# Decoder layer with a two-of-eight expert stage: reads of the first gathers' columns, the order of the last W2 loads, one expert's subtraction on GpSimd, and reads of tile numbers, moved

## The chip, the cores and the metric

The kernel runs on one core of one Trainium2 chip. The metric is the time on the device in microseconds (us). The engines are named as in the profile: PE (TensorE), PEld (its weight loads), DVE (VectorE), ACT (ScalarE), POOL (GpSimd) and SP (SyncE). SP issues most of the DMAs; POOL issues the gathers and scatters.

## The reference, cut to what matters

Eight batches of 256 rows of 256 numbers pass through three residual stages. The third one is the subject here.

```python
x = x + rbf_attention(layernorm(x))                 # self-attention, exp(-distance^2), softmax over it
x = x + cross_attention(ctx, ctx, layernorm(x))     # 16 heads, mask
xs = layernorm(x).reshape(-1, 256)                  # 2048 tokens
weights, sel = top_k(xs @ Wg, 2)                    # 2 of 8 experts for each token
weights = softmax(weights)
h = relu(einsum('td,edf->etf', xs, W1) + b1)        # W1: 8 x 256 x 1024
out_e = einsum('etf,efd->etd', h, W2) + b2          # W2: 8 x 1024 x 256
x = x + sum_k weights[k] * out_e[sel[k]]
```

## The kernel before

The program has an attention part and an expert part, and each engine's program is written out in the order in which it runs. The first part (`attention`) is called for steps -1 to 9. Each step works on several of the eight batches at different stages: scores of one batch, exponentials of the one before it, and so on. Steps 8 and 9 (`choosing` and `placing` in the code) have no new batch, and beside the last attention work they sort the tokens of the first five batches (10 groups of 128) into tiles of 128 rows for one expert each.

This sorting runs on DVE as a chain. `routing_table(core, eng, 0, c)` for c = 0 to 3 builds comparison matrices (L1800 to L1810, `local_hot`, `row_hot`, `local_vals`, `tile_vals`), nearly all of them from two inputs in SBUF. After each, PE multiplies them (`table_product`, L1561). The four PE products stand at fixed places between the attention's own products, and PE does nothing behind one of them until it has run. After the fourth, `routing_index` (L1823 to L1854) turns the sum into the rows to be gathered and raises the event `idx`.

The expert part (`experts`) has 39 tiles. Step n works on tile n-1 (the gathered rows are transposed, `ex_rows_t`, L2022), tile n-2 (times W1, `ex_hidden`, L2058 on PE; relu and rounding on ACT, L2068 and L2075; the rest after rounding, `hid_lo`, on DVE, L2078) and tile n-3 (times W2, `ex_out`, L2099). POOL gathers the rows of tiles 0 to 3 ahead (`ex_gather`, a copy L1993 and an indirect DMA L1996) and adds the results to the output one tile after another (`ex_scatter`, L2011). Step 0 to 17 are written out, then follows a loop. The second part of the tokens (the last three batches) is sorted in steps 3 to 11, beside the first tiles. `prefix_product` (L1551) in step 4 is the first PE instruction of it, and needs the choice of experts of the last batch, made on DVE (`st_router`, `st_best`, `routing_choice`; the last result is `both`, L1612).

A product with W2 takes W2 in two parts, the rounded number (`hi`) and what is left over (`lo`). Each expert's W2 (1 MB) is loaded by SP (`load_expert`, L490, in the order 0, 1, 2, 3, 7, 4, 5, 6, each one waiting for the load two before it), copied rounded by ACT (L1508) and subtracted by DVE (L1513) over 2048 numbers in each partition. The subtraction of expert 0 is done by POOL instead, in eight pieces of 256 (L1497), two in each of four attention steps. `ex_out` of tiles 0 to 2 waits for as many finished experts as the table `tile_splits` says, and tile 3 waits for all eight.

Which expert a tile has, which column of the table it uses and how many splits it needs is read from SBUF into a register (`value_load`, shown as TENSOR_LOAD in the lists below). An engine's following instructions wait in its program until the number is there. The reads stand right ahead of the instruction that uses the number.

## Time and profile before

| | |
|---|---|
| median of 3 runs | 641.94 us (641.94, 637.71, 984.14) |
| the profiled execution, its time | 641.79 us |
| its span, first to last instruction | 640.1 us |
| mean granted TensorE clock | 0.976 |
| PE busy | 583.3 us (91%) |
| DVE, ACT, POOL busy | 369.1, 333.6, 220.6 us |
| chain that ended last | PE 47%, DMA 31%, DVE 8%, issue 5% |

The attention part ends at about 354 us of the span, and the expert part fills the rest. "Granted clock" is the share of the full PE clock (1.00 is 2.4 GHz, 0.50 is 1.2 GHz). In the rows of a timeline the first number is the start of an instruction or a group in us from the span's start, the second its length in us; in brackets stands how long the engine was idle ahead of it and what ended that.

### The profile page before, as it was taken

What the parts mean: (1) busy time and instruction counts of PE and PEld (TensorE: products, weight loads), DVE (VectorE), ACT (ScalarE), POOL (GpSimd) and SP (SyncE); (2) the same over time, 40 slices, a digit from 0 to 9 for tenths busy, and PEclk for the clock granted to TensorE, in tenths of its full rate; (3) what the DMA queues carried; (4) which work ended last, traced back from release to release, by engine and by line L of the source; (5) the groups of instructions that cost most, each with busy time, mean ns of one, the idle gap of its engine ahead of it and who ended that gap; (6) DMA issues with size and microseconds to landing.
All of it is one profiled execution on the core that took longest, in us unless ns stands there. A gap on an engine that the chain in (4) does not pass through costs nothing.

```text
span 640.1 us, 15134 instructions
## 1 busy us (share of the span) xinstructions
PE 583.3 (91%) x4812; PEld 537.3 (84%) x4852; DVE 369.1 (58%) x920; ACT 333.6 (52%) x787; POOL 220.6 (34%) x283
## 2 busy tenths in 40 slices
PE   4666899999999999998968799999999999999991
PEld 3565888889798888977756799999999999999991
DVE  3636867778676767757868777565233332323331
ACT  4432364655547456453455664555656556565550
POOL 8322212212213121111002616443454655545532
PEclk9979999999999999999969899999999999999996
DMA  7383909063370907346157955666667676766732
GB/s 222 101 95 89 116 3 107 13 80 72 42 110 1 148 4 87 66 52 100 44 183 270 335 169 167 167 176 221 179 197 215 176 225 174 217 190 192 217 86 25
DMA packets 55430, 85.34 MB, mean 133 GB/s; under 512 B 6416, under 2 KB 44144, under 8 KB 55376
## 3 DMA queue, kind: packets, MB, share of 16 engines
q1 hardware_dynamic: 46368, 73.59, 48.3%
q0 software_dynamic: 7616, 10.26, 8.6%
q10 hardware_dynamic: 1392, 0.79, 0.4%
q8 instruction: 32, 0.52, 0.3%
q14 instruction: 22, 0.18, 0.1%
HBM read 62.44 MB, written 9.31 MB: 112 GB/s over the span
## 4 chain that ended last, share of the span: by engine, by line
PE 47%; DMA 31%; DVE 8%; issue 5%; ACT 2%; POOL 2%; POOLq 2%; SPq 1%; DVEq 0%; ACTq 0%
DMA out<-y,scatter_now 26%; PE bank L998 14%; PE bank L2058 5%; PE bank L1310 4%; PE bank L1253 4%; PE bank L1339 4%; PE bank L2099 4%; PE bank L1307 3%; PE bank L1250 3%; DMA q_stack<-cq_lo 2%; PE bank L964 2%; DMA exp_ring<-L_attn_Wo 1%; DMA experts_w<-L_ffn_W 1%; SPq L1081 1%; DMA slots_in<-xn_rows,gather_now 1%
## 5 line engine op out<-in xcount | busy, mean ns | idle before, releaser
L2058 PE MATMUL bank<-slots_t,w_now 128*128 128x128 f32 x1248 | 147.3, 277 | 0.0
L2058 PEld LDWEIGHTS bank<-slots_t,w_now 128*128 128x128 f32 x1248 | 144.0, 194 | 0.0
L2068 ACT ACTIVATE hid<-bank,b_tile 128x128 f32<-128x128 f32 x312 | 88.9, 368 | 55.1 <-PE bank L2058 55.1
L2011 POOL DMA_INDIRECT out<-y,scatter_now x39 | 63.7, 1633 | 119.4 <-DMA out<-y,scatter_now 77.5
L2078 DVE TENSOR_TENSOR hid_lo<-hid,hid_hi 128x1024 fp32r<-128x1024 f32 x39 | 47.8, 1226 | 97.1 <-ACT hid_hi L2075 97.1
L2099 PE MATMUL bank<-experts_w,hid_hi 128*128 x624 | 83.5, 285 | 2.5 <-ACT hid_hi L2075 1.5
L1261 DVE TENSOR_REDUCE row_max<-bank 128x2 f32<-128x512 f32 x128 | 81.0, 681 | 7.2 <-PE bank L1253 6.4
L1322 ACT ACTIVATE exp_ring<-bank 128x512 f32<-128x512 f32 x128 | 67.7, 605 | 26.3 <-PE bank L1310 26.3
L2099 PEld LDWEIGHTS bank<-experts_w,hid_hi 128*128 128x128 f32 x624 | 76.5, 188 | 2.8 <-issue 2.7
L1253 PE MATMUL bank<-k_stack,q_stack 96*128 96x256 f32 x256 | 67.3, 377 | 2.2 <-DMA q_stack<-cq_lo 2.2
L1310 PE MATMUL bank<-q_stack,k_stack 98*128 98x256 f32 x256 | 67.0, 382 | 0.0
L1310 PEld LDWEIGHTS bank<-q_stack,k_stack 98*128 98x128 f32 x256 | 51.3, 200 | 3.5
L1253 PEld LDWEIGHTS bank<-k_stack,q_stack 96*128 96x128 f32 x256 | 50.2, 196 | 3.5
L897 POOL TENSOR_SCALAR rstd<-moments 128x2 f32<-128x2 f32 x24 | 7.8, 326 | 128.7 <-DVE moments L894 128.7
L2075 ACT ACTIVATE hid_hi<-hid 128x512 fp32r<-128x512 f32 x78 | 49.3, 633 | 4.7
L1996 POOL DMA_INDIRECT slots_in<-xn_rows,gather_now x39 | 41.0, 1052 | 25.8 <-POOL gather_now L1993 15.4
L1993 POOL COPY gather_now<-gather_idx 128x1 uint32 x39 | 41.6, 1067 | 10.7 <-DVE jump L1854 10.7
L1307 PE MATMUL bank<-mask_k,ident_bf 128*128 128x512 bf16 x112 | 44.5, 398 | 0.0
L2099 PE MATMUL bank<-experts_w,hid_lo 128*128 x312 | 43.1, 280 | 0.0
L2028 ACT ACTIVATE slots_t<-bank 128x256 f32<-128x256 f32 x39 | 15.0, 384 | 53.5 <-PE bank L2022 53.5
L1250 PE MATMUL bank<-mask_q,ident_bf 128*128 128x512 bf16 x105 | 40.9, 390 | 0.1
L2099 PEld LDWEIGHTS bank<-experts_w,hid_lo 128*128 128x128 f32 x312 | 39.5, 188 | 0.0
(276 smaller groups left out, 1023.0 us busy)
## 6 DMA issues: line engine op xcount, KB each, us to landing
w_now<-L_ffn_W SPq DMA_DIRECT2D x39, 1024.0 KB
experts_w<-L_ffn_W SPq DMA_DIRECT2D x8, 1024.0 KB, 7.6
k_stack<-ck_hi SPq DMA_DIRECT2D x32, 128.0 KB, 4.6
q_stack<-cq_hi SPq DMA_DIRECT2D x32, 128.0 KB, 6.8
ctx_in<-ctx SPq DMA_DIRECT2D x8, 256.0 KB, 7.7
k_stack<-ck_lo SPq DMA_DIRECT2D x16, 128.0 KB, 4.8
q_stack<-cq_lo SPq DMA_DIRECT2D x16, 128.0 KB, 7.6
out<-x SPq DMA_DIRECT2D x7, 256.0 KB, 7.5
```

The costliest lines, as they stand in the source:

```text
L998: mm = eng.matmul(out, a, b, start=start and i == 0, stop=stop and i == len(terms) - 1, skip_group_check=skip)
L1250: eng.matmul(ps[:, :], core.ident_bf[:, :], core.mask_q[:, :, :], start=True, stop=False, skip_group_check=True)
L1253: mm = eng.matmul(ps[:, qt * S:(qt + 1) * S], q_stack[0:QROWS, c, i, qt * P:(qt + 1) * P], k_stack[0:QROWS, i, :], start=False, stop=True, ...
L1261: core.e["maxed"].at(eng.tensor_reduce(core.row_max[:, :, h], ps[:, :].rearrange("p (t k) -> p t k", t=KT), AX.X, ALU.max))
L1307: eng.matmul(ps[:, :], core.ident_bf[:, :], core.mask_k[:, :, :], start=True, stop=False, skip_group_check=True)
L1310: mm = eng.matmul(ps[:, kt * S:(kt + 1) * S], core.k_stack[b.p][0:rows, i, kt * P:(kt + 1) * P], core.q_stack[b.p][0:rows, c, i, :], start ...
L1322: core.e["exp"].at(eng.activation(core.exp_ring[:, n % 8, :, :], ps[:, :], ACT.Exp, scale=HD ** -0.5))
L2011: core.rows_out.at(eng.indirect_dma_start(core.out_rows, bass.IndirectOffsetOnAxis(ap=core.scatter_now[b.p][:, :], axis=0), core.y[b.p][:, ...
L2058: mm = eng.matmul(banks[half][:, f * P:(f + 1) * P], core.w1_now[b.p][:, c, start:start + P], core.slots_t[b.p][:, c, :], start=c == 0, st ...
L2068: act = eng.activation(core.hid[:, g, :], banks[half][:, f * P:(f + 1) * P], ACT.Relu, bias=core.b1_tile[b.p][:, g:g + 1])
L2075: core.m["hid_hi"].at(eng.activation(core.hid_hi[b.p][:, part, :], core.hid[:, part, :], ACT.Copy))
L2099: mm = eng.matmul(ps[:, 0:D], left[b.p][:, f, :], core.experts_w[:, bass.ds(x * PLACE + (part * FT * D + f * D), D)], start=term == 0 and ...
```

## The change

Four things are moved; none changes what is computed, and the count of heavy instructions is the same except that one subtraction of 2048 becomes eight of 256.

- POOL reads the columns of the first four gathers after the event `order` (raised in step 8) rather than one by one behind `idx`.
- SP loads W2 of expert 7 ahead of W1 of tile 1. The loads of W2 of experts 4, 5 and 6 wait until the gathers of tiles 0 and 1 have landed.
- W2 of expert 1 is subtracted on POOL in eight pieces in attention step 9, no longer on DVE behind `routing_index`. ACT's and DVE's work on W2 of expert 4 moves from step 2 and the head of step 3 to a place behind `ex_hidden` of tile 1, right ahead of that of expert 5.
- PE reads the tile's numbers for `ex_out` at the head of a step from 3 on (not in the loop).

```diff
--- before.py
+++ after.py
@@ -787,7 +787,10 @@
     exps(2, 2, 3, 4)
     at(0, st_rbf_out)
     if name == "gpsimd" and 3 <= it.v < 7:
-        split_first(core, eng, 2 * (it.v - 3))
+        split_piece(core, eng, 0, 2 * (it.v - 3))
+    elif name == "gpsimd" and placing:
+        for piece in range(PIECES):
+            split_piece(core, eng, 1, piece)
     exps(2, 5, 6)
     if choosing and name == "tensor":
         prefix_product(core, eng, 0)
@@ -825,7 +828,6 @@
         routing_table(core, eng, 0, 2)
         routing_table(core, eng, 0, 3)
         routing_index(core, eng, 0)
-        split_expert(core, name, eng, 1)
     scores(1, 4, 5)
     at(0, st_project, "cq")
     at(-1, st_transpose, "xnT")
@@ -857,7 +859,7 @@
         elif placing:
             split_expert(core, name, eng, 3)
     elif name == "gpsimd" and 3 <= it.v < 7:
-        split_first(core, eng, 2 * (it.v - 3) + 1)
+        split_piece(core, eng, 0, 2 * (it.v - 3) + 1)
     scores(0, 0, 1, 2)
     at(3, st_best)
     if choosing and name == "vector":
@@ -1461,11 +1463,13 @@
     e.wait_ge(core.r["order"], 1)
     e.wait_ge(core.E["residual_early"], 16 * EARLY_BATCHES)
     ex_load(core, "sync", e, Step(0, 0))
+    core.e["t_tile"].wait(e, LAST_BATCH)
+    load_expert(core, e, 7)
     e.wait_ge(core.r["table"], 4)
     ex_load(core, "sync", e, Step(0, 1))
-    core.e["t_tile"].wait(e, LAST_BATCH)
-    load_expert(core, e, 7)
     core.e["p_hT"].wait(e, LAST_BATCH)
+    for b in range(2):
+        core.rows_in.wait(e, Step(0, b))
     for x in (4, 5, 6):
         load_expert(core, e, x)
 
@@ -1489,11 +1493,11 @@
     return core.experts_w[:, start:start + FT * D]
 
 
-def split_first(core, eng, piece):
+def split_piece(core, eng, x, piece):
 
     width = FT * D // PIECES
-    hi, lo = (expert_part(core, 0, part)[:, piece * width:(piece + 1) * width] for part in range(2))
-    eng.wait_ge(core.w2["hi"], 1)
+    hi, lo = (expert_part(core, x, part)[:, piece * width:(piece + 1) * width] for part in range(2))
+    eng.wait_ge(core.w2["hi"], x + 1)
     rest = eng.tensor_tensor(lo, lo.bitcast(F32), hi.bitcast(F32), ALU.subtract)
     if piece == PIECES - 1:
         rest.then_inc(core.w2["lo"], 1)
@@ -1508,8 +1512,8 @@
         eng.activation(hi, lo.bitcast(F32), ACT.Copy).then_inc(core.w2["hi"], 1)
     elif name == "vector":
         eng.wait_ge(core.w2["hi"], n + 1)
-        if n == 1:
-            eng.wait_ge(core.w2["lo"], 1)
+        if n == 2:
+            eng.wait_ge(core.w2["lo"], 2)
         eng.tensor_tensor(lo, lo.bitcast(F32), hi.bitcast(F32), ALU.subtract).then_inc(core.w2["lo"], 1)
 
 
@@ -1871,9 +1875,11 @@
             at(0, ex_load)
     elif name == "gpsimd":
         if n == 0:
-            eng.wait_ge(core.r["idx"], 1)
+            eng.wait_ge(core.r["order"], 1)
+            core.columns = [column_of(core, eng, Step(b // 2, b % 2)) for b in range(4)]
             for b in (3, 4):
                 core.xn_stored.wait(eng, Step(b // 2, b % 2))
+            eng.wait_ge(core.r["idx"], 1)
         if n == FIRST:
             eng.wait_ge(core.r["idx"], 2)
             for b in (6, 7):
@@ -1891,6 +1897,10 @@
     elif name == "tensor":
         if n == 1:
             st_output(core, name, eng, LAST_BATCH, it)
+        if n is not None and n >= 3 and it.back(3).inside(MAX_TILES):
+            expert_of(core, eng, it.back(3))
+            if n < 6:
+                core.splits = splits_of(core, eng, it.back(3))
         at(1, ex_rows_t)
         at(2, ex_hidden)
         if n == 2:
@@ -1911,9 +1921,8 @@
         elif n == 4:
             split_expert(core, name, eng, 6)
         at(2, ex_hidden)
-        if n == 2:
+        if n == 3:
             split_expert(core, name, eng, 4)
-        elif n == 3:
             split_expert(core, name, eng, 5)
         if n == 2:
             store_residual(core, eng, LAST_BATCH)
@@ -1931,10 +1940,9 @@
             split_expert(core, name, eng, 3)
             st_normalise(core, name, eng, LAST_BATCH, it, 2)
             split_expert(core, name, eng, 7)
-        elif n == 3:
-            split_expert(core, name, eng, 4)
         at(2, ex_hidden)
         if n == 3:
+            split_expert(core, name, eng, 4)
             split_expert(core, name, eng, 5)
             st_router(core, name, eng, LAST_BATCH, it)
             st_best(core, name, eng, LAST_BATCH, it)
@@ -1968,6 +1976,10 @@
     return x
 
 
+def splits_of(core, eng, b):
+    return eng.value_load(core.tile_splits[0:1, bass.ds(b.v, 1)], min_val=1, max_val=NE)
+
+
 def tile_number(core, eng, b):
     return eng.value_load(core.tile_expert[0:1, bass.ds(b.v, 1)], min_val=0, max_val=NE - 1)
 
@@ -1989,7 +2001,7 @@
     rows, now = gather_buffers(core, b)
     before = b.back(4 if isinstance(b.v, int) and b.v < 6 else 2)
     core.rows_in.wait(eng, before, apart=core.apart)
-    g, col = column_of(core, eng, b)
+    g, col = core.columns[b.v] if isinstance(b.v, int) and b.v < 4 else column_of(core, eng, b)
     core.m["gnow"].at(eng.tensor_copy(now[:, :], core.gather_idx[g][:, bass.ds(col, 1)]))
     core.m["gnow"].wait(eng, b, apart=core.apart)
     core.m["xT"].wait(eng, before, apart=core.apart)
@@ -2084,8 +2096,7 @@
     if name == "tensor":
         x = expert_of(core, eng, b)
         if isinstance(b.v, int) and b.v < 3:
-            splits = eng.value_load(core.tile_splits[0:1, bass.ds(b.v, 1)], min_val=1, max_val=NE)
-            eng.wait_ge(core.w2["lo"], splits)
+            eng.wait_ge(core.w2["lo"], core.splits)
         elif isinstance(b.v, int) and b.v == 3:
             eng.wait_ge(core.w2["lo"], NE)
         core.m["hid_hi"].wait(eng, b)
```

The lists that follow show each engine's program by position, with the events that an instruction waits for. Line numbers of the changed kernel are 2 to 12 higher than those of the kernel before, and L2xxx, L1501 and L1517 there are the same code as L1497 and L1513 here.

POOL's program at the end of attention step 9, before. `rstd` is the last layernorm work of the attention steps (batch 6), `tile_col` the table of columns, `gather_now` and `slots_in` are the gather's index and its rows; the second to fourth gather repeat the last five rows.

```order
L897 TENSOR_SCALAR rstd<-moments 128x2 [waits e_ln2_stats]
L899 TENSOR_TENSOR rstd<-rstd,minus_half 128x2 [waits e_ln2_eps]
L1978 TENSOR_LOAD tile_col [waits xn_stored0,xn_stored1,r_idx]
L1978 ISA x2
L1993 ISA
L1993 COPY gather_now_154<-gather_idx_204 128x1
L1996 DMA slots_in_148<-xn_rows,gather_now_154 128x256 [waits m_gnow]
```

The same place in the changed kernel.

```order
L899 TENSOR_SCALAR rstd<-moments 128x2 [waits e_ln2_stats]
L901 TENSOR_TENSOR rstd<-rstd,minus_half 128x2 [waits e_ln2_eps]
L1501 TENSOR_TENSOR experts_w<-experts_w 128x256 [waits w2_hi] x8
L1990 TENSOR_LOAD tile_col [waits r_order]
L1990 ISA x2
...
L1990 TENSOR_LOAD tile_col
L1990 ISA x2
L2005 ISA [waits r_idx,xn_stored0,xn_stored1]
L2005 COPY gather_now_154<-gather_idx_204 128x1
L2008 DMA slots_in_148<-xn_rows,gather_now_154 128x256 [waits m_gnow]
```

Eight pieces of the subtraction now stand between the layernorm work and the gathers, four reads of `tile_col` (two of them shown) behind them, and `idx` is waited for only ahead of the copy.

DVE's program in expert steps 2 and 3, before, without the reads of tile numbers. The `experts_w` rows are, from the top, the subtractions of experts 4 and 5; `hid_lo_214` and `hid_lo_215` belong to tiles 0 and 1; `logits`, `top_54` and `idx_55` to the choice of the last batch.

```order
L2078 TENSOR_TENSOR hid_lo_214<-hid,hid_hi_134 128x1024 [waits m_hid_hi]
...
L2044 COPY b_tile_152<-b_cols 128x8
L1513 TENSOR_TENSOR experts_w<-experts_w 128x2048 [waits w2_hi]
L2078 TENSOR_TENSOR hid_lo_215<-hid,hid_hi_135 128x1024 [waits m_hid_hi]
L1513 TENSOR_TENSOR experts_w<-experts_w 128x2048 [waits w2_hi]
L1436 COPY logits<-bank 128x16 [waits e_p_gate]
L1592 MAX top_54<-logits 128x8 [waits e_gate]
L1592 MAX top_54<-logits 128x8
L1595 MAX_INDEX idx_55<-top_54,logits 128x8 [waits e_best] x2
```

And in the changed kernel.

```order
L2090 TENSOR_TENSOR hid_lo_214<-hid,hid_hi_134 128x1024 [waits m_hid_hi]
...
L2056 COPY b_tile_152<-b_cols 128x8
L2090 TENSOR_TENSOR hid_lo_215<-hid,hid_hi_135 128x1024 [waits m_hid_hi]
L1517 TENSOR_TENSOR experts_w<-experts_w 128x2048 [waits w2_hi] x2
L1438 COPY logits<-bank 128x16 [waits e_p_gate]
L1596 MAX top_54<-logits 128x8 [waits e_gate]
L1596 MAX top_54<-logits 128x8
L1599 MAX_INDEX idx_55<-top_54,logits 128x8 [waits e_best] x2
```

The subtraction of expert 4 has gone from ahead of tile 1's `hid_lo` to behind it, so that both stand between it and the last batch's choice. On ACT the rounding of expert 4 moves in the same way, from behind tile 0's `hid_hi` to behind tile 1's.

PE's program from the end of step 2 to the first `ex_out`, before. L1416 is the transposing of the last batch's `xn_ffn` for the router, L1431 the router, the `ident,slots_in` rows transpose tile 2, `slots_t_151,w_now` is tile 1 times W1.

```order
L1416 MATMUL bank<-ident,xn_ffn 128x128 [waits e_ln2,e_hT_lo]
...
L2022 MATMUL bank<-ident,slots_in_142 128x128 [waits m_slots_t,rows_in2]
L2022 MATMUL bank<-ident,slots_in_142 128x128
L2058 MATMUL bank<-slots_t_151,w_now_213 128x128 [waits m_slots_t,w1_in1]
L2058 MATMUL bank<-slots_t_151,w_now_213 128x128 x15
L1431 MATMUL bank<-gate_w,xf_t 128x8 [waits e_xfT]
...
L1972 TENSOR_LOAD tile_expert
L1972 ISA x2
L2087 TENSOR_LOAD tile_splits
L2087 ISA x2
L2099 ISA [waits m_hid_hi,w2_lo]
```

And in the changed kernel.

```order
L1418 MATMUL bank<-ident,xn_ffn 128x128 [waits e_ln2,e_hT_lo]
...
L1984 TENSOR_LOAD tile_expert
L1984 ISA x2
L1980 TENSOR_LOAD tile_splits
L1980 ISA x2
L2034 MATMUL bank<-ident,slots_in_142 128x128 [waits m_slots_t,rows_in2]
L2034 MATMUL bank<-ident,slots_in_142 128x128
L2070 MATMUL bank<-slots_t_151,w_now_213 128x128 [waits m_slots_t,w1_in1]
L2070 MATMUL bank<-slots_t_151,w_now_213 128x128 x15
L1433 MATMUL bank<-gate_w,xf_t 128x8 [waits e_xfT]
...
L2110 ISA [waits m_hid_hi,w2_lo]
```

The two reads have moved from between the router and tile 0's product with W2 to ahead of tile 2's transposes. The steps behind it are changed in the same way.

## Rows read from the trace of the kernel before

**Rows 1.** Busy time by stretch: us, PE, PEld, DVE, ACT, POOL, PEclk, DMA share, GB/s

```profile
320.00:330.00 10.00, 4.24 (x26) 3.93 (x26) 5.02 (x26) 4.56 (x4) 0.00 (x0) 0.65 0.54 176
330.00:340.00 10.00, 10.00 (x73) 7.90 (x76) 9.83 (x31) 5.98 (x12) 1.60 (x2) 0.84 0.81 246
500.00:620.00 120.00, 120.00 (x1053) 120.00 (x1052) 39.77 (x73) 69.34 (x199) 62.13 (x70) 1.00 0.68 192
```

**Rows 2.** Timeline in the loop: PE, the W1 products of two tiles that follow each other

```profile
505.18 3.74 PE L2058 MATMUL bank<-slots_t,w_now 128*128 128x128 f32 x32
...
511.80 3.74 PE L2058 MATMUL bank<-slots_t,w_now 128*128 128x128 f32 x32
```

**Rows 3.** Timeline, DVE, the last three routing tables of step 9 and what follows

```profile
335.76 1.55 DVE L1810 TENSOR_TENSOR tile_vals<-onehot,local_vals 128x400 fp32r<-128x400 f32 x3
337.22 0.73 DVE L917 TENSOR_SCALAR xn_ffn<-x,moments,rstd 128x256 f32<-128x256 f32 x2
...
342.12 1.55 DVE L1810 TENSOR_TENSOR tile_vals<-onehot,local_vals 128x400 fp32r<-128x400 f32 x3
...
345.82 0.17 DVE L1854 COPY jump<-taken 128x8 f32<-128x8 f32 x1
345.90 2.29 DVE L1513 TENSOR_TENSOR experts_w<-experts_w 128x2048 fp32r<-128x2048 f32 x1
```

**Rows 4.** Timeline, PE, the third and fourth table product

```profile
341.20 0.72 PE L1561 MATMUL bank<-tile_vals,row_hot 128*128 128x240 f32 x5
...
343.73 0.82 PE L1561 MATMUL bank<-tile_vals,row_hot 128*128 128x240 f32 x5 [0.38 <-DVE tile_vals L1810]
```

**Rows 5.** Line L1497 (POOL's pieces of expert 0), and POOL's last attention instruction

```profile
L1497 POOL TENSOR_TENSOR experts_w<-experts_w x8: 716/726/741, 125.9 to 256.8; 128x256 fp32r<-128x256 f32 x8
...
335.53 0.78 POOL L899 TENSOR_TENSOR rstd<-rstd,minus_half 128x2 f32<-128x2 f32 x1
```

**Rows 6.** Timeline, places where POOL and DVE both read SBUF with two inputs

```profile
25.86 1.27 POOL L925 TENSOR_TENSOR x<-x,bias_attn_bo 128x512 f32<-128x512 f32 x1 [5.66 <-DVE bias_attn_bo L688]
26.22 1.45 DVE L628 TENSOR_TENSOR xattnWvl<-exp_ring,xattnWvh 128x512 fp32r<-128x512 f32 x1
...
27.60 0.68 DVE L628 TENSOR_TENSOR xattnWol<-exp_ring,xattnWoh 128x512 fp32r<-128x512 f32 x1
...
347.00 1.24 POOL L1993 COPY gather_now<-gather_idx 128x1 uint32 x1 [10.70 <-DVE jump L1854]
```

**Rows 7.** Timeline, PE: one product at the low clock, the last attention product, tiles 0 and 1

```profile
329.21 0.63 PE L998 MATMUL bank<-xattnWoh,tr_hi 128*128 128x256 f32 x2
...
352.99 0.40 PE L998 MATMUL bank<-xattnWoh,tr_lo 128*128 128x256 f32 x2
...
354.11 0.44 PE L2022 MATMUL bank<-ident,slots_in 128*128 128x128 f32 x2 [0.71 <-DMA slots_in<-xn_rows,gather_now]
...
356.02 0.44 PE L2022 MATMUL bank<-ident,slots_in 128*128 128x128 f32 x2 [1.48 <-DMA slots_in<-xn_rows,gather_now]
```

**Rows 8.** Chain that ended last, in order of time: tile 1's gather

```profile
350.14 5.84 DMA slots_in<-xn_rows,gather_now
```

**Rows 9.** Timeline of all engines, from the last batch's layernorm to tile 1's W2 product

```profile
359.05 0.73 DVE L917 TENSOR_SCALAR xn_ffn<-x,moments,rstd 128x256 f32<-128x256 f32 x2 [0.94 <-POOL rstd L899]
...
368.45 2.26 PE L2099 MATMUL bank<-experts_w,hid_hi 128*128 x16 [1.55 <-ACT hid_hi L2075]
...
368.82 0.63 ACT L2075 ACTIVATE hid_hi<-hid 128x512 fp32r<-128x512 f32 x1
369.36 1.90 ACT L1508 ACTIVATE experts_w<-experts_w 128x2048 fp32r<-128x2048 f32 x1
...
374.97 0.21 DVE L1612 TENSOR_TENSOR both<-onehot 128x48 f32<-128x48 f32 x1
...
376.86 2.46 PE L2099 MATMUL bank<-experts_w,hid_hi 128*128 x16 [0.92 <-issue]
```

**Rows 10.** DMA issues of 356 to 360 us: the last W2 load, KB, us to landing

```profile
experts_w<-L_ffn_W SPq DMA_DIRECT2D x1, 1024.0 KB, 6.4
```

## The prediction

> **What bounds the kernel now.** I read the busy time by stretch first, to see which engine is full where. From 500 to 620 us PE is busy throughout at a granted clock of 1.00 [rows 1], and two W1 products of tiles that follow each other start 6.62 us apart [rows 2]: in the expert part PE sets the pace, and a us that the first tiles start earlier or later is a us at the end. In the 20 us from 320 PE is neither full nor at its full clock (4.24 of 10 us busy, clock 0.65, then 0.84) [rows 1]. So I read the timelines of all engines from there to about 380 us, where everything that the change touches stands.
>
> Three waits of PE are what the change is about. (a) Tile 0's and tile 1's transposes wait 0.71 and 1.48 us for gathered rows [rows 7]; tile 1's gather takes 5.84 us to land [rows 8]. (b) Tile 0's product with W2 starts 1.55 us after PE's last work, where two numbers are read; for tile 1 the gap is 0.92 us [rows 9]. (c) Ahead of both, PE's third and fourth table product depend on DVE: the fourth starts at 343.73, 0.38 us late, right behind DVE's last `tile_vals`, which end at 343.67 [rows 3, 4].
>
> **Reading the columns ahead.** DVE raises `idx` at 345.99, POOL's first copy starts at 347.00 and ends at 348.24 [rows 3, 6]. The read costs about 1.0 us there. The copy itself, of one number in each partition, takes 1.24 us because DVE's subtraction of expert 1 runs from 345.90 to 348.19 [rows 3]: POOL is let through when that ends. With both gone a copy would end near 346.3, and the gathers start up to 1.9 us earlier. What this can give is bounded by wait (a): 0.71 + 1.48 = 2.2 us on PE.
>
> **W2 loads behind the gathers.** They leave the gathers more of the DMA engines. The last W2 load takes 6.4 us to land [rows 10]. Loads 4 and 5 would start when tile 1's rows are in, at the latest at 356.0 in before's time [rows 8], and 6 when 4 is in, so all have landed by about 356.0 + 2 x 6.4 = 368.8. ACT needs 4 only after tile 1's `hid_hi`, which ends at 369.45 now [rows 9]. I cost this at nothing; if the loads took twice as long, ACT's splits would be up to 5 us late.
>
> **The eight pieces on POOL.** This is the term that decides. They stand behind `rstd`, which ends at 336.31 [rows 5], and take 0.726 us each [rows 5], 5.8 us together. POOL is idle then, so by busy time they are free. But DVE has no gap between 335.76 and 343.67 [rows 3], and nearly all of it is comparisons and products with two inputs in SBUF. What happens when both engines do that is seen at 26.22: a DVE subtraction that takes 0.68 us when it is alone takes 1.45 us, while POOL's L925 runs until 27.13 [rows 6]. DVE lost 0.77 us of the 0.91 us that POOL still had. Eight pieces taken in turn with DVE's instructions then cost DVE 0.726 - 0.14 = 0.59 us each, 4.7 us; taken one behind the other 5.8 us. I take 5.3. PE waits for these very tables, and its other work cannot pass a table product, so PE's fourth table product, `idx` and all behind them are 5.3 us later.
>
> One row speaks against it: POOL's `rstd` power (335.53 to 336.31, two SBUF inputs of two numbers) runs beside three `tile_vals` from 335.76, which take their usual 1.55 us [rows 3, 5]. It reads only two numbers, and a piece reads 256, as L925 reads 512; I side with L925.
>
> The Trainium skill (SBUF — State Buffer, "Who interferes with whom") says that a DVE instruction with two SBUF inputs and a GpSimd instruction that reads SBUF exclude each other for the whole instruction, whichever starts first. The row at 26.22 agrees and the row at 335.53 does not. By this rule alone the term would be the full eight pieces, 5.8 us, and by the row at 335.53 alone nothing.
>
> **The clock.** In the 20 us in which PE first idled the granted clock was 0.65 and 0.84 [rows 1]; the same pair of products takes 0.63 us at the low level (1.2 GHz) and 0.40 at 2.4 GHz [rows 7]. PE's third table product can now start 5.3 us later than 341.20 [rows 4], an idle stretch like that one. Between the fourth table product and the last attention product, 343.73 to 353.39 [rows 4, 7], PE has some 6 us of work on the path, with waits for ACT and DVE between. At the low clock throughout it grows by up to 4.9 us (0.8 of it); if the clock stays high, nothing. I take 1.7, about a third of the work at the low level.
>
> **DVE without expert 1's subtraction.** It ended at 348.19 [rows 3], 0.15 us ahead of which `r_heads` could have run: -0.15 us.
>
> **From the last attention product to tile 1's W2 product** (353.39 to 376.86 [rows 7, 9]). With the rows there in time, tile 0's W1 product starts 1.7 us earlier: transposes, ACT's copy and transposes take 1.2 us, where it is 2.9 us now. But what PE does next, transposing the last batch's `xn_ffn`, waits for DVE, which ends that at 359.78 [rows 9], and no part of the change moves this. Behind it stand now the two reads, 1.5 us by the gap in (b), so that tile 2's transposes and tile 1's W1 product start 0 to 0.5 us earlier than now. Gain (a) ends there. ACT finishes tile 1's `hid_hi` 1.7 to 2.1 us earlier than 369.45 [rows 9], since expert 4 is not ahead of it. Then come ACT's roundings of 4 and 5 (1.90 us each [rows 9]), and DVE's subtractions (2.29 us each [rows 3]) with the choice of the last batch behind both. In sum: 367.3 to 367.8, two roundings later 371.1 to 371.6; DVE's first subtraction ends at 371.5 to 372.0, the second at 373.8 to 374.3, `both` 1.6 us later at 375.4 to 375.9, against 375.18 now. PE's prefix product waits for it, takes 0.76, and tile 1's product with W2 follows without the gap, at 376.2 to 376.7, against 376.86. So gains (a) and (b), 2.2 + 1.55 + 0.92 = 4.7 us as they stand in the rows, shrink to about 0.4 us: what is late next is DVE with expert 4 and 5 ahead of the choice.
>
> **Reads further on.** From tile 2 on the gaps are not there, since PE has products queued; they cost nothing before and nothing after. The loop is not touched.
>
> **Sum.** 5.3 + 1.7 - 0.15 - 0.4 = +6.45 us. The profiled execution's 641.79 (span 640.1) is 0.15 below the median, so the median should be 641.94 + 6.45 = 648.4 us. With the low ends, 4.7 + 0 - 0.15 - 0.65, it is 645.8, with the high ends, 5.8 + 4.9 - 0.15 - 0.2, 652.3.
>
> **Rivals.**
> 1. DVE is not held up: both read side by side as at 335.53, or DVE always goes first and POOL's pieces fill its gaps. Side by side: -0.15 - 0.4 gives 641.4 us. DVE first: the pieces start at 343.7, end near 349.6, and tile 1's gather lands about 1.5 us later than 355.98, of which the wait for `xn_ffn` takes most; about 642.5 us. For it speaks the row at 335.53, against it 26.22 and the copy at 347.00. 0.20.
> 2. Faster: DVE is not held up and the order around experts 4 and 5 costs less than I think, because ACT gets to tile 1 earlier than by my chain. Then (a), (b) and (c) count, up to 4.7 + 0.38: 636.9 us. It decides if `both` comes before 374. Even this is within 2% of before. 0.07, of which 0.01 is over 2%.
> 3. Slower by over 2% (above 654.8): the loads of W2 behind the gathers are late as well. It needs the high sum and another 2.5 us, as when load 4 takes 13 us or more. The DMA engines are less loaded then than now. 0.04.
> 4. The forecast, DVE held up: 0.69.
>
> **Numbers.** 648.4 us. The forecast's own range is 645.8 to 652.3. Rival 1 has to be taken in with its larger part, so the range is 641.0 to 652.5. Chances: faster by over 2% 0.01, within 2% 0.94, slower by over 2% 0.05 (2% is about what a measurement of this kernel can tell from no change).
>
> **What would show it.** In the changed profile: the routing chain's `tile_vals` and `row_hot` on DVE are longer than 1.55 and 0.82 us while POOL runs its pieces, or the gaps between them are; PE waits some 5 us ahead of the third table product and the granted clock falls there; `idx` comes near 351.3; tiles 0 and 1 no longer wait for rows; no gap ahead of tile 0's W2 product; `both` ends later than PE's W1 product of tile 2 and PE waits for it. If `tile_vals` take 1.55 and the third product starts near 341.2, the main step is wrong and the time is that of rival 1 or 2.

## The result and the profile after

| | before | after |
|---|---|---|
| median of 4 runs each | 640.39 us (637.71, 638.85, 641.94, 984.14) | 649.60 us (648.15 to 651.16) |
| ratio | | 1.0148, 95% interval 1.0122 to 1.0174 |
| profiled execution, its span | 640.1 us | 649.2 us |
| mean granted TensorE clock | 0.976 | 0.961 |

The changed kernel is 1.5% slower. The median of before still counts its run of 984.14 us, of which nothing on record says the cause; the ratio goes by fast runs alone, so without it. In all later runs the kernel before took 640.2 to 641.0 us in the median. The forecast was 648.4 us, with a range from 641.0 to 652.5, and "within 2%".

First the timeline of after, DVE and POOL, in the stretch that answers to [rows 3, 5]. The columns are start, length, engine, line, operation, output and inputs, count, and in brackets idle time and what ended it.

```profile
337.08 2.08 DVE L1814 TENSOR_TENSOR tile_vals<-onehot,local_vals 128x400 fp32r<-128x400 f32 x3
339.08 1.57 DVE L919 TENSOR_SCALAR xn_ffn<-x,moments,rstd 128x256 f32<-128x256 f32 x2
340.57 0.74 DVE L1804 TENSOR_TENSOR local_hot<-iota_f,slot_tile 128x50 f32<-128x50 f32 x1
341.23 1.38 DVE L1806 TENSOR_TENSOR row_hot<-iota_f,slot_row 128x640 fp32r<-128x640 f32 x1
342.54 0.74 DVE L1811 TENSOR_TENSOR local_vals<-local_hot,token_f 128x50 f32<-128x50 f32 x1
...
344.67 1.55 DVE L1814 TENSOR_TENSOR tile_vals<-onehot,local_vals 128x400 fp32r<-128x400 f32 x3
346.25 0.21 DVE L1804 TENSOR_TENSOR local_hot<-iota_f,slot_tile 128x50 f32<-128x50 f32 x1
346.38 0.82 DVE L1806 TENSOR_TENSOR row_hot<-iota_f,slot_row 128x640 fp32r<-128x640 f32 x1
...
337.60 6.97 POOL L1501 TENSOR_TENSOR experts_w<-experts_w 128x256 fp32r<-128x256 f32 x8
```

POOL's eight pieces run from 337.60 to 344.57. As long as they do, `tile_vals` takes 2.08 us and not 1.55, `xn_ffn` 1.57 and not 0.73, `row_hot` 1.38 and not 0.82. `local_hot` takes 0.74 in place of the 0.21 that it has at 346.25, and so do the three `local_vals` (0.20 alone). The group behind the last piece, at 344.67, takes 1.55 again. The excesses add up to 0.53 + 0.84 + 0.53 + 0.56 + 3 x 0.55 = 4.1 us. `xn_ffn`, which has only one tensor as input, lost the most of any group.

Next the timeline of PE in after, which answers to [rows 4, 7, 9], with the two DVE rows that end PE's wait for `both`.

```profile
346.27 1.42 PE L1565 MATMUL bank<-tile_vals,row_hot 128*128 128x240 f32 x5 [3.33 <-DVE tile_vals L1814]
...
350.13 1.25 PE L1565 MATMUL bank<-tile_vals,row_hot 128*128 128x240 f32 x5
...
361.10 0.63 PE L1000 MATMUL bank<-xattnWoh,tr_lo 128*128 128x256 f32 x2
...
362.73 0.42 PE L2034 MATMUL bank<-ident,slots_in 128*128 128x128 f32 x2 [0.57 <-ACT slots_t L2040]
...
369.12 0.56 PE L2034 MATMUL bank<-ident,slots_in 128*128 128x128 f32 x2 [1.03 <-issue]
369.47 5.26 PE L2070 MATMUL bank<-slots_t,w_now 128*128 128x128 f32 x32
...
378.41 4.50 DVE L1517 TENSOR_TENSOR experts_w<-experts_w 128x2048 fp32r<-128x2048 f32 x2 [0.58 <-ACT experts_w L1512]
...
384.28 0.21 DVE L1616 TENSOR_TENSOR both<-onehot 128x48 f32<-128x48 f32 x1
...
384.64 0.39 PE L1555 MATMUL bank<-both,strict 128*128 128x48 f32 x2 [2.40 <-DVE both L1616]
...
385.08 2.84 PE L2110 MATMUL bank<-experts_w,hid_hi 128*128 x16
387.72 1.91 PE L2110 MATMUL bank<-experts_w,hid_lo 128*128 x8
```

PE waits 3.33 us ahead of the third table product and 2.40 us for `both`, which stands behind both subtractions (experts 4 and 5, 4.50 us) on DVE. The rows of tiles 0 and 1 are there when they are wanted, and tile 0's product with W2 follows without its gap of 1.55 us. But the last product of the attention part takes 0.63 and not 0.40, and tile 1's W1 products 5.26 and not 3.74. Before has a slow group of its own, though, one tile earlier, behind its waits for the rows of tiles 0 and 1:

```profile
356.30 5.37 PE L2058 MATMUL bank<-slots_t,w_now 128*128 128x128 f32 x32
```

In after tile 0's W1 products take 3.74 us, so each kernel has one such group at the low clock in its profile, and the two nearly cancel. The busy time by stretch (columns as in [rows 1]) has the clock:

```profile
343.00:353.00 10.00, 6.73 (x43) 5.25 (x48) 7.10 (x19) 2.37 (x5) 1.56 (x3) 0.66 0.43 139
...
370.00:375.00 5.00, 5.00 (x36) 5.00 (x35) 0.82 (x2) 2.00 (x7) 1.78 (x2) 0.73 1.02 360
...
386.00:390.00 4.00, 4.00 (x23) 4.00 (x22) 2.68 (x5) 0.01 (x1) 1.59 (x1) 0.57 0.35 141
```

The granted clock is at the low level (1.2 GHz) for part of each of these stretches: behind the wait for the third table, behind the wait for `xn_ffn` and the gap of 1.03 us, and behind the wait for `both`.

A balance by landmarks of the two profiled executions, after minus before, shows where the difference arises:

| landmark | before | after | difference | new in this stretch |
|---|---|---|---|---|
| end of the first table's `tile_vals` | 332.93 | 334.25 | +1.32 | +1.32 (ahead of all that was changed) |
| end of the fourth table's `tile_vals` | 343.67 | 349.14 | +5.47 | +4.15 |
| start of the fourth table product | 343.73 | 350.13 | +6.40 | +0.93 |
| end of the last attention product | 353.39 | 361.73 | +8.34 | +1.94 |
| start of tile 0's W2 product | 368.45 | 375.38 | +6.93 | -1.41 |
| start of tile 1's W2 product | 376.86 | 385.08 | +8.22 | +1.29 |
| start of tile 2's W2 product | 383.81 | 393.28 | +9.47 | +1.25 |
| end of the span | 640.1 | 649.2 | +9.1 | -0.4 |

Behind tile 2's product nothing is gained or lost any more: as forecast, PE sets the pace there.

The first row is the play between executions. The code ahead of the first table is the same in before, after, e1 to e6 and e8, and their first table ends anywhere from 331.76 us (e2) to 335.97 (e6).

### The profile page after: what moved, and what is told of

The parts are those of the page before. It is cut to its first block, busy times and chain, and to the rows that moved or that the text cites. A ratio compares the mean times of both kernels' runs of the same rounds, so it can differ in the third digit from the quotient of the medians.

```text
span 649.2 us, 15142 instructions
## 1 busy us (share of the span) xinstructions
PE 592.2 (91%) x4812; PEld 544.1 (84%) x4852; DVE 372.5 (57%) x919; ACT 333.4 (51%) x787; POOL 226.9 (35%) x291
## 4 chain that ended last, share of the span: by engine, by line
PE 77%; DVE 7%; DMA 6%; POOL 3%; issue 2%; ACT 2%; SPq 2%; POOLq 0%; DVEq 0%; ACTq 0%
PE bank L2070 20%; PE bank L2110 16%; PE bank L1000 13%; PE bank L1255 5%; PE bank L1312 5%; PE bank L1341 4%; PE bank L1309 4%; DMA q_stack<-cq_lo 3%; PE bank L1252 3%; PE bank L966 2%; SPq L1083 2%; PE bank L2034 1%; POOL q_stack L594 1%; DMA experts_w<-L_ffn_W 1%; PE bank L1565 1%
## 5 line engine op out<-in xcount | busy, mean ns | idle before, releaser
L1255 PE MATMUL bank<-k_stack,q_stack 96*128 96x256 f32 x256 | 69.3, 385 | 2.8 <-DMA q_stack<-cq_lo 2.8
L1312 PE MATMUL bank<-q_stack,k_stack 98*128 98x256 f32 x256 | 68.5, 388 | 0.0
L1255 PEld LDWEIGHTS bank<-k_stack,q_stack 96*128 96x128 f32 x256 | 51.7, 202 | 3.9
L2005 POOL COPY gather_now<-gather_idx 128x1 uint32 x39 | 40.3, 1034 | 8.7 <-DVE jump L1858 8.6
```

Source lines behind the costliest of these rows:

```text
L1255: mm = eng.matmul(ps[:, qt * S:(qt + 1) * S], q_stack[0:QROWS, c, i, qt * P:(qt + 1) * P], k_stack[0:QROWS, i, :], start=False, stop=True, ...
L1312: mm = eng.matmul(ps[:, kt * S:(kt + 1) * S], core.k_stack[b.p][0:rows, i, kt * P:(kt + 1) * P], core.q_stack[b.p][0:rows, c, i, :], start ...
```

## The experiments

The tables below give each kernel's ratio to the kernel before that ran on the same chip. Two lengths are read from each profile, since executions differ by up to 4.2 us already at the first table, with the same code up to there: **D**, from the end of the first table's `tile_vals` to the end of the fourth's, which is DVE's chain (10.74 in before, 14.89 in after), and **R**, from the start of the fourth table product to the start of tile 2's product with W2 (40.08 and 43.15). Each profile is one execution. D is the same to 0.04 us in all nine without pieces or fills on POOL. R is not as firm: which products fall into the low clock changes it by one to two us a group, and the times of before alone spread over 7 us (637.7 to 644.5). Where R and the times disagree, the times decide.

### e1 to e3: the change in parts

e1 is before with POOL's pieces alone.

```
     at(0, st_rbf_out)
...
+    elif name == "gpsimd" and placing:
+        for piece in range(PIECES):
+            split_piece(core, eng, 1, piece)
...
         routing_index(core, eng, 0)
-        split_expert(core, name, eng, 1)
```

> The kernel before with one part of the change: expert 1 is subtracted on POOL in eight pieces in step 9 and no longer on DVE; everything else as before. Theory (DVE is held up by the pieces): the third and fourth routing tables end 4 to 5.8 us later against the first one than in the kernel before, PE idles ahead of its third table product and its clock falls to 0.50, and the time is 6 to 8 us over before. Rival (both engines read side by side, the loss sits elsewhere in the change): tables as before, time within 1 us of before.

e2 is the changed kernel with expert 1 back on DVE (the diff above, backwards).

> The changed kernel with expert 1 subtracted on DVE behind the index as before; all other parts of the change stay. Theory: the routing tables end as in the kernel before, no idle stretch of PE there, and the time is that of before or up to 0.5 us less, 9 us under the changed kernel; PE waits ahead of the prefix product, since DVE's experts 4 and 5 stand in front of the last batch's choice. Rival (the loss comes from the late W2 loads or from the new order of expert 4): the time stays within 2 us of the changed kernel.

e3 is e2 with ACT's and DVE's work on expert 4 back at its old places (DVE's part is shown).

```
 vector:
+        elif n == 3:
+            split_expert(core, name, eng, 4)
         at(2, ex_hidden)
         if n == 3:
-            split_expert(core, name, eng, 4)
             split_expert(core, name, eng, 5)
```

> As the run without pieces, and the work on expert 4 is back where it was before on ACT and on DVE; what stays of the change are the columns read ahead, the W2 loads behind the gathers and PE's reads ahead. Theory: the choice of the last batch comes earlier against tile 0, PE no longer waits some 2 us ahead of the prefix product, and the time is 1.5 to 2.5 us under the run without pieces, so about 2 us under before. Rival (the order of expert 4 does not matter, another wait takes over): within 0.5 us of the run without pieces.

| | median us (before 640.18) | ratio | 95% interval | D | R |
|---|---|---|---|---|---|
| e1, pieces alone | 644.83 | 1.0069 | 1.0041 to 1.0098 | 14.87 | 37.33 |
| e2, all but the pieces | 642.41 | 1.0023 | 1.0004 to 1.0042 | 10.74 | 42.51 |
| e3, all but pieces and order of 4 | 639.99 | 0.9989 | 0.9965 to 1.0014 | 10.74 | 37.53 |

The pieces alone cost 0.7%, 4.4 us, less than the 6 to 8 that I expected. D is as long as in after with them and as in before without: the whole +4.15 us is theirs. The timeline of PE in e1:

```profile
346.34 1.35 PE L1563 MATMUL bank<-tile_vals,row_hot 128*128 128x240 f32 x5 [4.18 <-DVE tile_vals L1812]
...
350.02 0.72 PE L1563 MATMUL bank<-tile_vals,row_hot 128*128 128x240 f32 x5
...
366.80 3.74 PE L2060 MATMUL bank<-slots_t,w_now 128*128 128x128 f32 x32
...
370.37 0.96 PE L1433 MATMUL bank<-gate_w,xf_t 128*128 128x8 f32 x8
371.29 2.29 PE L2101 MATMUL bank<-experts_w,hid_hi 128*128 x16
```

The same wait as in after stands there, but tile 1's W1 products run at the full clock (3.74 us; 5.26 in after), and the time is 5 us less than after's.

Two more things are seen here. R is 2.75 us shorter than in before: expert 1's subtraction no longer stands between the index and POOL's first copy, the waits for the rows of tiles 0 and 1 are 0.58 and 0.56 us in place of 0.71 and 1.48, and tile 0's W1 products run at the full clock. And tile 0's product with W2 follows the router with no gap, though PE's reads stand where they stood in before. So before's 1.55 us is no fixed price of two reads. In before ACT finishes `xf_t`, which the router needs, at 365.79 and the router starts at 365.84; in e1 `xf_t` is ready 1.1 us ahead of it. That PE comes to the reads late because its router product came late fits both rows, but no run changes that alone.

What the order of expert 4 costs is seen between e2 and e3. The timelines of PE, first e2 and then e3:

```profile
352.80 0.63 PE L998 MATMUL bank<-xattnWoh,tr_lo 128*128 128x256 f32 x2
...
361.48 5.06 PE L2068 MATMUL bank<-slots_t,w_now 128*128 128x128 f32 x32
...
376.46 0.39 PE L1553 MATMUL bank<-both,strict 128*128 128x48 f32 x2 [2.40 <-DVE both L1614]
...
376.90 2.95 PE L2108 MATMUL bank<-experts_w,hid_hi 128*128 x16
379.65 1.86 PE L2108 MATMUL bank<-experts_w,hid_lo 128*128 x8
```

```profile
363.34 3.74 PE L2070 MATMUL bank<-slots_t,w_now 128*128 128x128 f32 x32
...
374.78 0.39 PE L1553 MATMUL bank<-both,strict 128*128 128x48 f32 x2 [0.16 <-DVE both L1614]
...
375.22 2.25 PE L2110 MATMUL bank<-experts_w,hid_hi 128*128 x16
377.31 1.10 PE L2110 MATMUL bank<-experts_w,hid_lo 128*128 x8
```

With expert 4 behind tile 1's `ex_hidden`, `both` is 2.40 us late to the hundredth as in after, and the W2 product behind the wait runs at the low clock (2.95 + 1.86 against 2.25 + 1.10). With expert 4 at its old place the wait is 0.16. By R the order costs 5.0 us in these two executions, of which some 1.3 are tile 1's W1 products at the low clock (5.06); by the times it is 0.34%, 2.2 us, give or take 2. The size is open between these, the sign is not. Both runs missed what I expected of them against before: e2 is 0.2% slower (expected: the same or up to 0.5 us less), e3 is no faster (expected: 2 us).

The parts (4.4 and 1.5 us) add up to 5.9 us, and the whole is 9.4. On top of e2 the pieces cost 1.2% (1.0148 / 1.0023), 8 us (7.2 by the medians), where on top of before they cost 4.4. The two R's say what the difference may be: on before the pieces gave back 2.75 us of R, as told above, and on e2, where the other moves have taken those waits away already, they give back nothing (42.51 and 43.15). That is 3.4 us of the 3.5, from one execution of each, and so a reading and not a proof. The low clock differs too: in after it holds over the fourth table product (1.25 us, in e1 0.72) and over the last attention products (0.63, in e1 0.40). The latter is not the pieces' doing alone, since e2 has 0.63 there without any.

### e4: does POOL's reading or its writing hold DVE up?

The pieces are replaced by pairs of fills, 0.6 us a pair, that read nothing.

```
-            split_piece(core, eng, 1, piece)
+            write_piece(core, eng, piece)
```

`write_piece` fills 387 numbers of `table` and 256 of W2's `lo` part with zeros. The small rest of expert 1's W2 is left out.

> The changed kernel with POOL writing zeros in the pieces' place instead of subtracting: eight times two fills (387 and 256 numbers), with no SBUF input, so that the small rest of expert 1's W2 is left out. Theory (DVE is held up because both read SBUF): the routing tables take their usual 1.55 us beside POOL's fills, PE has no idle stretch ahead of the third table product, and the time is within 1 us of the run without pieces. Rival (any work of POOL in that place holds DVE up, or the writes do): tables late by 3 us and more and the time within 3 us of the changed kernel.

Measured: 647.06 us, ratio 1.0095, 1.0059 to 1.0130; D 14.49. The time misses the theory, by which it would be that of e2 (642.41). The timeline of DVE and POOL:

```profile
336.77 1.55 DVE L1827 TENSOR_TENSOR tile_vals<-onehot,local_vals 128x400 fp32r<-128x400 f32 x3
338.23 4.47 DVE L920 TENSOR_SCALAR xn_ffn<-x,moments,rstd 128x256 f32<-128x256 f32 x2
...
337.26 0.42 POOL L1513 MEMSET table<- 128x387 f32 x1
...
341.93 0.31 POOL L1514 MEMSET experts_w<- 128x256 f32 x1
```

Two answers. `tile_vals`, with two inputs in SBUF, runs beside the fills from 337.26 in its usual 1.55 us, where beside the reading pieces it took 2.08: for the two-input instructions it is POOL's reading that counts. (This one group is all that the run has of it.) But `xn_ffn`, with one tensor input, stands from 338.23, where the fourth of the sixteen fills starts, until the last is over at 342.24, 4.47 us in place of 0.73. It is not let in between two fills, although in after it was held up by 0.84 us only. So DVE's chain is late by 3.75 us by another way, and the time says nothing on the reads; the rows do.

The Trainium skill (SBUF — State Buffer, "Who interferes with whom") states both halves: a two-input DVE instruction contends with GpSimd's reads and not with its writes, while a `tensor_scalar` in its two-port mode contends with either. The `tile_vals` rows agree with the first half. `xn_ffn` fits the second, held up by fills and by reading pieces alike, if it runs in that mode, which no row shows. That it waits through thirteen instructions in a row is not in the Trainium skill's rule, by which each instruction holds the ports for its own length.

### e8: half as many pieces

Before, with four pieces of expert 1 on POOL and its second half (1024 numbers) on DVE behind the index.

```
+        for piece in range(PIECES // 2):
+            half_piece(core, eng, piece)
...
-        split_expert(core, name, eng, 1)
+        other_half(core, eng)
```

> e1 with half the dose: before, with the first four of the eight pieces of expert 1 on POOL and the second half of that expert (1024 numbers in each partition) on DVE behind the index. If each piece costs DVE its 0.55 us (held up one by one), DVE's last tile_vals and PE's fourth table product are 2.2 us later than in before, idle time of PE ahead of the third product about 1.2 us, and the time about 2 us above before (642 to 643; e1 was 4.6 above). If what costs is one long stall or the low clock behind the 3.3 us of idle time, it is disproportionate: under 0.5 us for four pieces, or as much as e1.

Measured: 642.25 us (before 640.61), ratio 1.0036, 1.0008 to 1.0063; D 12.66, R 37.54. Its timeline:

```profile
335.93 2.08 DVE L1832 TENSOR_TENSOR tile_vals<-onehot,local_vals 128x400 fp32r<-128x400 f32 x3
337.94 1.55 DVE L921 TENSOR_SCALAR xn_ffn<-x,moments,rstd 128x256 f32<-128x256 f32 x2
...
340.07 0.81 DVE L1824 TENSOR_TENSOR row_hot<-iota_f,slot_row 128x640 fp32r<-128x640 f32 x1
```

D grows by 1.92 us with four pieces and by 4.13 with eight: 0.48 and 0.52 us for a piece. `row_hot`, which now comes behind the last piece, takes its usual 0.81. The price on DVE goes by the number of pieces that meet it, as the forecast had it. In time they cost 0.4% and 0.7%, in the order expected, though the intervals overlap.

### e5, e6: the parts that were costed at little or nothing

e5 is before with PE's reads of the tile numbers at the head of the step.

```
+        if n is not None and n >= 3 and it.back(3).inside(MAX_TILES):
+            expert_of(core, eng, it.back(3))
+            if n < 6:
+                core.splits = splits_of(core, eng, it.back(3))
         at(1, ex_rows_t)
```

> The kernel before with one part alone: PE reads the tile's expert and its number of splits at the head of the step, not ahead of tile 0's product with W2. If my term for it holds (the wait of 1.55 us ahead of tile 0's product goes, but `both` is unchanged and PE waits for it instead, behind tile 0's product), the time is 0 to 0.5 us below before, 640 us, and PE has a wait of 0.5 to 1.5 us for `both`. If all that is seen in the gap is gained (1.55 + 0.92), 2.5 us below. If the reads cost as much at the head of the step, where tile 2's transposes now stand behind them, no difference at all and a gap of 0.9 us there.

e6 is e3 with SP's old order of loads.

```
+    e.wait_ge(core.r["table"], 4)
+    ex_load(core, "sync", e, Step(0, 1))
     core.e["t_tile"].wait(e, LAST_BATCH)
     load_expert(core, e, 7)
-    e.wait_ge(core.r["table"], 4)
-    ex_load(core, "sync", e, Step(0, 1))
     core.e["p_hT"].wait(e, LAST_BATCH)
-    for b in range(2):
-        core.rows_in.wait(e, Step(0, b))
```

> e3 (columns ahead, reads ahead on PE, experts 1 and 4 at their old places) with SP's old order: W2 of expert 7 behind W1 of tile 1, experts 4, 5 and 6 without waiting for the gathers of tiles 0 and 1. If the waiting of the loads does nothing for PE, as I costed it, the time is that of e3 within 0.3% and tile 1's gather still lands ahead of PE's transposes. If the loads took DMA engines from the gathers, tile 1's transposes wait again for rows, 1 to 1.5 us, but ACT has experts 4 and 5 earlier; up to 1 us either way.

| | median us (before 640.61) | ratio | 95% interval | R |
|---|---|---|---|---|
| e5 | 639.84 | 0.9978 | 0.9948 to 1.0008 | 39.12 |
| e6 | 640.14 | 1.0010 | 0.9981 to 1.0039 | 37.66 |

The timeline of PE in e5:

```profile
361.11 0.60 PE L2030 MATMUL bank<-ident,slots_in 128*128 128x128 f32 x2 [1.04 <-issue]
...
367.38 2.14 PE L2106 MATMUL bank<-experts_w,hid_hi 128*128 x16
...
374.44 0.39 PE L1551 MATMUL bank<-both,strict 128*128 128x48 f32 x2 [0.19 <-DVE both L1612]
```

The gap of 1.55 us ahead of tile 0's W2 product is gone and one of 1.04 us stands ahead of tile 2's transposes, where the forecast put it. PE waits only 0.19 us for `both`, where I expected 0.5 to 1.5. R is 1.0 us shorter; the times don't tell it from nothing. e6's R is e3's within 0.13 us: the new order of loads gives and takes nothing here, as forecast. e6's PE does wait 0.92 us for tile 1's rows (e3: none), but the wait for `xn_ffn` behind it is shorter for that (0.37 us, in e3 0.80).

### e7, e10: what stands ahead of the tables

In before PE waits 5.20 us ahead of the first table, for `tr_lo`, whose `tr_hi` stands on ACT behind the rounding of expert 1, and that waits 5.01 us for its load. The timeline of before, PE and ACT (rows not shown so far):

```profile
327.79 0.77 PE L998 MATMUL bank<-xattnWoh,tr_hi 128*128 128x256 f32 x2 [5.20 <-DVE tr_lo L988]
...
324.27 1.91 ACT L1508 ACTIVATE experts_w<-experts_w 128x2048 fp32r<-128x2048 f32 x1 [5.01 <-DMA experts_w<-L_ffn_W]
...
326.35 0.57 ACT L977 ACTIVATE tr_hi<-bank 128x512 fp32r<-128x512 f32 x1
```

e7 moves that rounding behind `max_hi` and `tr_hi`, the next one into step 9, and SP's load of expert 2 behind that of the maxima (only the first is shown).

```
-    if choosing and name == "scalar":
-        split_expert(core, name, eng, 1)
     at(1, st_maxima)
     at(2, st_transpose, "hT")
...
         elif choosing:
-            split_expert(core, name, eng, 2)
+            split_expert(core, name, eng, 1)
```

> The kernel before, with another edit: ACT's rounding of expert 1 moved behind `max_hi` and `tr_hi` in step 8, that of expert 2 behind the last exponential of step 9, and SP's load of expert 2 behind the maxima's. It tests where the time ahead of the routing tables comes from: in every profile PE waits 3.5 to 5.2 us near 325 us for tr_lo, whose tr_hi stands on ACT behind the rounding of expert 1, which waits for its load. If that load is the cause, the wait goes (PE starts the product 3 to 5 us earlier, all tables too, no low clock at 330), and the time is 3 to 6 us below before: 634 to 637 us. If PE then only waits for the maxima or for the exponentials instead, 0 to 2 us below.

e10 is e7 with the pieces.

> e7 (ACT's roundings of experts 1 and 2 and the load of 2 moved) with the eight pieces of expert 1 on POOL. In e7 DVE's chain of tables alone sets PE's pace from 328 us: PE waits 0.23 to 0.67 us ahead of all four table products, where in before only the fourth waits 0.38. If the pieces hold DVE up by 4.1 us as in e1, PE has no slack of its own to give: the fourth product is 4.1 us later than e7's 339.28 and the time is 4 to 5 us above e7's 638.4 (642.5 to 643.5), and the four pieces' share of the low clock comes on top. If e1's cost came only from the state that PE was in behind its low clock near 330, less than 3 us above e7.

| | median us | ratio | 95% interval | D | R |
|---|---|---|---|---|---|
| e7 (before 640.61) | 638.44 | 0.9967 | 0.9940 to 0.9994 | 10.75 | 41.38 |
| e10 (before 640.75) | 643.91 | 1.0053 | 1.0034 to 1.0072 | 14.85 | 38.37 |

The timeline of PE in e7:

```profile
323.34 0.47 PE L998 MATMUL bank<-xattnWoh,tr_hi 128*128 128x256 f32 x2 [1.50 <-DVE tr_lo L988]
...
339.28 0.83 PE L1561 MATMUL bank<-tile_vals,row_hot 128*128 128x240 f32 x5 [0.67 <-DVE tile_vals L1810]
...
352.87 0.69 PE L2022 MATMUL bank<-ident,slots_in 128*128 128x128 f32 x2 [2.54 <-DMA slots_in<-xn_rows,gather_now]
```

The load was the cause: the wait is 1.50, as it is in all five kernels with this edit. The fourth table product starts 4.45 us earlier than in before, but the time is only 2.1 us less, where I expected 3 to 6. Before's profile was an unlucky one in this place: the eight other kernels that have the old order wait 3.5 to 3.9 us there and not 5.20, so that the edit saves some 2.0 to 2.4 us. And DVE's chain now sets the pace of all four tables, and tile 1's gather has become the wait, 2.54 us. With the pieces (e10) D is 4.10 longer again, and e10 is 0.86%, 5.5 us, above e7, against 4.4 for e1 above before. So the pieces cost no less when PE comes to the tables early and at the full clock (that they cost more is not shown, the intervals allow for either). It is DVE's delay that costs; PE waits 4.18 us for the third table there, and the low clock follows.

### e11 to e13: a version that is faster than both

e11 joins e3 and e7 and puts PE's reads behind `ex_hidden`, under the 32 W1 products. Its expectation was 635.5 us.

```
         at(1, ex_rows_t)
         at(2, ex_hidden)
+        if n is not None and n >= 3 and it.back(3).inside(MAX_TILES):
+            expert_of(core, eng, it.back(3))
```

> e3 with e7's edit, and PE's reads of the tile numbers one place further down: behind the 32 products of ex_hidden and ahead of the router. If e3's columns and loads are worth what tile 1's gather loses in e7 (2.54 us of waiting for rows), and the reads run under the W1 products there (the gap of 1.03 us ahead of tile 2's transposes goes, and none comes ahead of tile 0's product with W2), the time is 2 to 4 us below e7's 638.4, about 635.5. If the reads are still in the way, the gap stands ahead of the router or of tile 0's product and it is 637.

e12 is e11 with expert 1 subtracted on DVE in two halves, where DVE waits for others.

```
+        half_expert(core, eng, 1, 0)
         routing_index(core, eng, 0)
-        split_expert(core, name, eng, 1)
...
     at(3, st_router)
+    if placing and name == "vector":
+        half_expert(core, eng, 1, 1)
```

> e11 with the subtraction of expert 1 on DVE in two halves (1024 numbers in each partition, 1.23 us each as in e8), one between the last tile_vals and routing_index, where DVE waits 1.2 us for PE, the other behind the first copy of logits, where it waits 1.4 us for ACT; in all kernels so far the whole of it, or the pieces, stand on the path or hold up POOL's first copy. If both halves fit into these waits, the first gather starts 1.5 to 2 us earlier, none of the tiles 0 to 2 waits for rows, heads and tr_lo are no later, and the time is 0 to 1 us below e11. If a half is longer than its wait, tr_lo is up to 0.5 us later and the time the same as e11.

e13 is e12 with W1 of tile 2 ahead of the last W2 load (and no longer issued in step 2).

```
-    for x in (4, 5, 6):
+    for x in (4, 5):
         load_expert(core, e, x)
+    ex_load(core, "sync", e, Step(1, 0))
+    load_expert(core, e, 6)
```

> e12 with one DMA moved on SP's queue: W1 of tile 2 is issued ahead of the load of W2 of expert 6, no longer behind it. In e12 PE waits 2.26 us for that W1 (it was issued at 355.82 and needed at 364.4) and runs tile 2's W1 products at the low clock behind the wait (5.46 us in place of 3.74). If the load of 6 in front of it is the cause, W1 is there in time, the products take 3.74, and the time is 3 to 4 us below e12, 633 to 634. If the DMA engines themselves are full (342 to 420 GB/s in that stretch) and W1 lands late all the same, or expert 6 is late for tile 3, 0 to 1.5 us below.

| | median us | ratio | 95% interval | R |
|---|---|---|---|---|
| e11 (before 640.75) | 638.45 | 0.9974 | 0.9955 to 0.9992 | 38.79 |
| e12 (before 640.75) | 636.65 | 0.9930 | 0.9908 to 0.9952 | 39.11 |
| e13 (before 640.99) | 637.07 | 0.9940 | 0.9919 to 0.9962 | 36.03 |

The timeline of e12, DVE, POOL and PE:

```profile
339.67 1.22 DVE L1512 TENSOR_TENSOR experts_w<-experts_w 128x1024 fp32r<-128x1024 f32 x1
340.94 0.41 DVE L1838 COPY table<-bank 128x240 f32<-128x240 f32 x1
...
342.35 0.19 POOL L2018 COPY gather_now<-gather_idx 128x1 uint32 x1 [9.96 <-DVE jump L1869]
...
366.63 5.46 PE L2083 MATMUL bank<-slots_t,w_now 128*128 128x128 f32 x32 [2.26 <-DMA w_now<-L_ffn_W]
```

e12 is 0.7% (4.5 us) faster than before and, by the ratios (0.9930 / 1.0148), 2.1% faster than the changed kernel. The halves fit into DVE's waits: the first ends at 340.89 and the table's copy starts at 340.94. POOL's first copy takes 0.19 us and not 1.24, since DVE runs nothing beside it. Why e12 takes 0.4% less than e11 the profiles do not show. From the fourth table product to the last attention product both take 9.67 us, R is no shorter, and the lead that e12 has in the profile, 1.8 us, stands ahead of the first table, where the code is the same. What the rows show is that the halves cost nothing.

e11 missed its expectation: it is no faster than e7. The reads do run under the W1 products, and no gap of 1.03 us is left ahead of tile 2's transposes. But PE waits 2.12 us for W1 of tile 2 (2.26 in e12), whose issue stands on SP's queue behind the W2 loads that wait for the gathers, and its products follow at the low clock. Here PE does wait for a load that stands behind the others, which it did not in e6 and in after. The timeline of PE in e13:

```profile
367.00 3.73 PE L2085 MATMUL bank<-slots_t,w_now 128*128 128x128 f32 x32
371.61 0.39 PE L1568 MATMUL bank<-both,strict 128*128 128x48 f32 x2 [0.88 <-DVE both L1629]
```

The wait for W1 is gone, the products take 3.73, R is 3.1 us shorter, and yet the times of e12 and e13 cannot be told apart, where I expected 3 to 4 us. In the profiled execution e13's first table came 2.9 us later than e12's (331.91 against 329.01), ahead of all that differs in the code, and such a difference is within the play between executions (4.2 us). Why nothing of the 3.1 us shows in the times is open.

## Why the prediction was right, step by step

- **PE sets the pace in the expert part**: right. From tile 2 on the two profiles run in parallel, 0.4 us apart at the end.
- **The eight pieces hold DVE up, +5.3**: the mechanism was right, as e1, e8 and e10 show, and rival 1 (side by side, or DVE first) is out. The size was too large: D grew by 4.15 us, below even my low end of 4.7. The term that was mis-sized is "eight pieces at 0.59 us each": DVE lost 0.53 to 0.56 us for each instruction that met a piece, and in the two groups of several instructions (three `tile_vals`, two `xn_ffn`) only 0.53 and 0.84. That makes 0.52 us for a piece. POOL lost as well: its pieces took 0.87 us each and not 0.726. The step reckoned with instructions of two SBUF inputs; that `xn_ffn`, with one tensor, would be held up too (and most of all) was not in it.
- **The clock, +1.7**: right in kind, too small in sum. The third table product started 5.1 us later than in before (346.27 against 341.20; 1.3 of it is the first row of the balance), and the granted clock fell. Behind it PE lost 0.93 us up to the fourth product and 0.77 us from there to the wait for `tr_lo`, together the 1.7 of the forecast. The six products behind that wait ran at the low clock too, another 1.17 us; e2, e3 and e5 have this without any late table, so it is not the wait for the table that brings it. And the clock fell behind the wait for `both`, +1.25 us from tile 1's to tile 2's W2 product, which no term held.
- **`r_heads` earlier, -0.15**: too small to be seen.
- **The columns ahead**: right. From the end of `jump` to POOL's first copy 1.01 us pass in before and 0.27 in after (352.92 to 353.19), and the copy takes 0.19 us.
- **Gains (a) and (b) shrink to 0.4 us**: right in the sum. From the end of the last attention product to tile 1's W2 product before takes 23.47 us and after 23.35. The rows are in time, the gap has moved ahead of tile 2's transposes at 1.03 us, and PE waits for `both` as said, 22.76 us behind the last attention product where I had 22.0 to 22.5. Part of this is luck: the forecast held no W1 group at the low clock in after, which has one (5.26 us), and did not count that before had one as well (5.37). What the step did not say is how much would have been left with expert 4 at its old place (e3's R is 5.0 us shorter than e2's, its time 2.2 us). And it took the gap of 1.55 us for the price of two reads, which e1 shows it is not always.
- **Loads at nothing**: right for this kernel (e6). In a faster one (e11) PE waits 2.12 us behind them.
- **Sum**: the stretches give 4.15 + 0.93 + 1.94 - 0.12 + 1.25 = 8.15 us, where the forecast had 6.45. The first table's 1.32 us and the end's -0.4 make it 9.1. The measured difference of the medians is 9.2 us. That the forecast's 648.4 came within 1.2 us of the median is luck in good part. The pieces were put too high and the clock too low, and the median it started from, 641.94, stood above what before takes in all later runs (640.2 to 641.0).
- **Rival 3** (over 2%, late loads) did not come: what was added to the forecast's sum was the clock, and the loads were not late.

## What to carry to other kernels

Work given to an engine that is idle is not free when it reads SBUF beside a chain of two-input instructions on DVE, and above all when PE waits for that chain: look for waits of the loaded engine itself first, and split the work to fit them, as e12 did without a loss. Moving a wait on PE is worth little if the next one is as near: read which engine stands behind each of them, the queue of the issuing engine too. A new idle stretch of PE has to be counted with the products that may follow it at 1.2 GHz, not just with its own length: behind the waits of 2.12 us (e11) to 5.20 us (before) they did, behind the 1.50 us for `tr_lo` in some executions and not in others. And one profile of each kernel is not enough to price a wait: before's 5.20 us was 3.5 to 3.9 in eight others.
